# Windowed attention in fp32: edge windows in two groups instead of three, softmax sums inverted on ScalarE by exp and log

## The reference

```python
xn  = layer_norm(x)                              # over the 192 channels
win = pad(xn, 16x16 -> 28x28), cut into 14x14 windows   # 4 windows an image, 196 tokens each
q, k, v = win @ qkv_w                            # 12 heads of 16 channels
s   = (q * 16**-0.5) @ k.T + rel_h(q)[.., :, None] + rel_w(q)[.., None, :]
out = softmax(s, axis=-1) @ v
x   = x + out @ proj_w + proj_b
x   = x + gelu(layer_norm(x) @ fc1_w + fc1_b) @ fc2_w + fc2_b
```

## Time and profile before

| | |
|---|---|
| three runs | 332.98, 334.4, 335.4 us; median 334.4 |
| the profiled execution | 337.13 us; its span in the profile 335.3 us |
| granted clock of TensorE, mean | 0.98 |
| busy share of the span | PE 95%, DVE 57%, ACT 43%, POOL 30% |
| chain that ended last | PE 86%, DVE 7%, ACT 4%, DMA 2% |
| attention blocks in the span | about 7 to 142 us and 163 to 300 us |

### The profile page before, as it was taken

How to read it: one execution, slowest core, us unless ns; L and a number is a source line. 1 busy time by engine, 2 the same in 40 slices (tenths; PEclk the granted TensorE clock), 3 DMA queues, 4 the chain that set the end, 5 groups by cost and what they waited for, 6 DMA issues and landing times.

```text
span 335.3 us, 9323 instructions
## 1 busy us (share of the span) xinstructions
PE 319.6 (95%) x3886; PEld 239.4 (71%) x3886; DVE 190.3 (57%) x457; ACT 143.7 (43%) x312; POOL 102.0 (30%) x215
## 2 busy tenths in 40 slices
PE   6999997999998999999999999799999899999997
PEld 3447686887876439977855769578887644998576
DVE  4473784877867400136674578587785920335572
ACT  3277136554556522024247515655455455002430
POOL 3000553487551049100000066277663104000000
PEclk9599998999999999999999999799999999999999
DMA  7973000000031103020021100000000000000002
GB/s 203 383 269 68 15 7 16 8 10 5 5 86 43 25 0 118 2 70 2 0 96 20 37 4 12 14 9 6 5 4 3 3 0 0 2 0 2 0 2 94
DMA packets 10268, 13.81 MB, mean 41 GB/s; under 512 B 3505, under 2 KB 8337, under 8 KB 10226
## 3 DMA queue, kind: packets, MB, share of 16 engines
q1 hardware_dynamic: 9602, 13.12, 12.5%
q10 hardware_dynamic: 624, 0.09, 0.2%
HBM read 10.95 MB, written 0.79 MB: 35 GB/s over the span
## 4 chain that ended last, share of the span: by engine, by line
PE 86%; DVE 7%; ACT 4%; DMA 2%; issue 1%; ACTq 0%; DVEq 0%
PE banks L1034 13%; PE banks L1006 12%; PE banks L1128 10%; PE banks L1146 9%; PE banks L962 6%; PE banks L1054 6%; PE banks L925 6%; PE banks L896 3%; PE banks L1312 2%; PE banks L885 2%; PE banks L1159 2%; PE banks L1206 2%; PE banks L938 2%; DMA slot_cols<-in_slot_cols 2%; ACT arena L1398 1%; PE banks L1176 1%
## 5 line engine op out<-in xcount | busy, mean ns | idle before, releaser
L1398 ACT ACTIVATE arena<-banks 128x392 f32<-128x392 f32 (+1 forms) x120 | 50.0, 469 | 44.0 <-PE banks L1034 44.0
L1585 DVE TENSOR_REDUCE negmax<-banks 128x4 f32<-128x784 f32 (+1 forms) x52 | 46.7, 897 | 17.5 <-PE banks L1006 17.0
L1006 PE MATMUL banks<-attention_arena 32*128 32x196 f32 x384 | 50.7, 365 | 0.9 <-DVE negmax L1581 0.4
L1034 PE MATMUL banks<-attention_arena 32*128 32x196 f32 x384 | 48.8, 351 | 0.4 <-ACT arena L1398 0.4
L1034 PE MATMUL banks<-attention_arena,keys 32*128 32x196 f32 x384 | 45.7, 332 | 0.0
L1006 PE MATMUL banks<-keys,attention_arena 32*128 32x196 f32 x384 | 45.5, 331 | 0.0
L1034 PEld LDWEIGHTS banks<-attention_arena 32*128 32x128 f32 x384 | 31.5, 191 | 7.0 <-issue 5.2
L1128 PE MATMUL banks<-yT,fc 128*128 128x512 f32 (+1 forms) x96 | 33.3, 607 | 0.0
L1006 PEld LDWEIGHTS banks<-keys,attention_arena 32*128 32x128 f32 x384 | 33.0, 190 | 0.0
L1034 PEld LDWEIGHTS banks<-attention_arena,keys 32*128 32x128 f32 x384 | 33.0, 190 | 0.0
L1006 PEld LDWEIGHTS banks<-attention_arena 32*128 32x128 f32 x384 | 29.9, 190 | 3.7 <-DVE negmax L1581 1.9
(11 more groups left out here) (181 smaller groups left out, 583.2 us busy)
## 6 DMA issues: line engine op xcount, KB each, us to landing
fc<-in_fc SPq DMA_DIRECT2D x2, 768.0 KB, 5.0
fc<-in_fc SPq DMA_DIRECT2D x2, 576.0 KB, 5.6
attention_arena<-negmaxT SPq DMA_DIRECT2D x68, 1.0 KB
rel<-in_rel SPq DMA_DIRECT2D x2, 448.0 KB, 5.9
x_tok<-in_x SPq DMA_DIRECT2D x4, 192.0 KB, 4.4
inverse<-in_inverse SPq DMA_DIRECT2D x1, 768.0 KB
inverse<-in_space_back SPq DMA_DIRECT2D x1, 768.0 KB, 3.9
qkv<-in_qkv SPq DMA_DIRECT2D x1, 576.0 KB, 3.8
```

The lines of the kernel that those rows point to most:

```text
L1006: ins = mm(o, asking, asked, start=not with_rel, stop=bool(with_rel))
L1034: last = mm(m.bank[4 + j][key_rows(b), cols * tile:cols * (tile + 1)], keys_of(slot, b, j, tile)[with_rel], queries_of(slot, b, j, tile)[w ...
L1398: run(m.probsT[keys, n % P_RING, j, 0:cols], m.bank[4 + j][keys, 0:cols], ACT.Exp).then_inc(s.probs, 1)
L1585: dve.tensor_reduce(at[rows, 4 * part:4 * part + 4].rearrange("k (j a) -> k j a", a=2), m.banks[rows, 2 * part:2 * part + 2, 0:2 * keys].r ...
```

## The change

1. **Edge groups.** The six edge units make two groups of three units (`PER_GROUP`), so there are 14 groups: n = 8 and 9 are edges, n = 10 to 13 slot 2. An edge group's `turn` and `score` have six steps, its `weigh` 12 matmuls; matmuls in all are as many as before. `OUT_AT` follows, and the projections stand in the same order as before.
2. **Inverse on ScalarE.** `take_logs` takes Ln of the SBUF copy with a scale and a bias per partition, which leaves the logarithm of the sum in the sum rows and 0 in the others; `invert` takes Exp of minus that, with a bias of 0 or -1e30 per partition. VectorE's `move_inverses` is one stream shuffle that swaps the 16-row halves. So value rows hold the inverse and the other rows 0, and GpSimd's masking goes: `divide` has one instruction for slots 0 and 2, two for slot 1. An edge group with units of both kinds has Ln and Exp in two parts.
3. **Tables.** One set with Exp and Ln is preloaded per attention block; the root of the norm becomes Exp(-0.5 Ln(var)), and VectorE's reciprocal goes. Gelu's table stays.
4. **Padding rows later.** VectorE turns at the end of n = 1, takes maxima at n = 2, sums at n = 3, adds at n = 4, turns back in the middle of n = 5; ScalarE's padding exponential stands at the end of n = 2, the logarithm at the end of n = 3; GpSimd's `shift_pads` behind `divide(0)`, `pad_rows` behind `divide(2)`.
5. **Loads.** `slot_cols` gets a semaphore of its own; TensorE's first transposes wait for `ident` alone.

```diff
 GROUPS = [(slot, b) for slot in range(2) for b in range(IMAGES)]
-GROUPS += [(slot, EDGES) for slot in range(SLOTS)]
+GROUPS += [(third, EDGES) for third in range(UNITS // PER_GROUP)]
 GROUPS += [(SLOTS - 1, b) for b in range(IMAGES)]
...
+def key_tiles(b):
+    return 2 if b < EDGES else PER_GROUP
+def steps_of_group(n):
+    return 2 * key_tiles(GROUPS[n][1])
...
+        def value_parts(n):
+            if GROUPS[n][1] < EDGES:
+                return [(VALUE_HALF[GROUPS[n][0]], slice(0, 1))]
+            own = [[at for at, u in enumerate(units(n)) if VALUE_HALF[unit_slot(u)] == half] for half in range(2)]
+            return [(half, slice(at[0], at[-1] + 1)) for half, at in enumerate(own)]
...
                 edge(0)
-                shift_pads()
                 edge(1)
-                pad_rows()
                 for n in range(N_GROUPS):
                     divide(n)
+                    if n == 0:
+                        shift_pads()
+                    elif n == 2:
+                        pad_rows()
                     if n == 1:
                         edge(2)
...
-                    pe.wait_ge(ident_loaded, 16 * 2)
+                    pe.wait_ge(ident_loaded, 16)
...
             def root(ln, g):
                 act.wait_ge(ln.stats, variances_taken(g))
-                run(m.std[:, 4 * g:4 * g + 4], m.var[:, 4 * g:4 * g + 4], ACT.Sqrt).then_inc(ln.std, 1)
+                own = slice(4 * g, 4 * g + 4)
+                run(m.std[:, own], m.var[:, own], ACT.Ln).then_inc(ln.std, 1)
+                act.wait_ge(ln.std, logged(g))
+                run(m.rstd[:, own], m.std[:, own], ACT.Exp, scale=-0.5).then_inc(ln.std, 1)
...
-                load_table(ACT.Sqrt)
+                act.preload_act_table_set("natural_log_exp_and_others")
...
+                def take_logs(n):
+                    act.wait_ge(s.pv_out, n + 1)
+                    for half, at in value_parts(n):
+                        ins = run(in_parts(m.log[:, n % 2], n)[:, at], in_parts(m.o[:, n % 2], n)[:, at], ACT.Ln,
+                                  scale=c["slot_cols"][:, SLOTS + 1 - half:SLOTS + 2 - half], bias=c["slot_cols"][:, SLOTS + half:SLOTS + half + 1])
+                    ins.then_inc(s.inverted, 1)
+                def invert(n):
+                    act.wait_ge(s.inverted, sums_logged(n))
+                    if n >= 2:
+                        act.wait_ge(s.inverses_moved, n - 1)
+                    for half, at in value_parts(n):
+                        ins = run(in_parts(m.recip[:, n % 2], n)[:, at], in_parts(m.log[:, n % 2], n)[:, at], ACT.Exp, scale=-1.0,
+                                  bias=c["slot_cols"][:, 2 * SLOTS + 1 + half:2 * SLOTS + 2 + half])
+                    ins.then_inc(s.inverted, 1)
...
                         for j in (2 * pair, 2 * pair + 1):
                             run(m.probsT[keys, n % P_RING, j, 0:cols], m.bank[4 + j][keys, 0:cols], ACT.Exp).then_inc(s.probs, 1)
+                            if n > 0 and j == 2 and not last_scored(n):
+                                take_logs(n - 1)
                         if n > 0 and pair == last_scored(n):
                             take_weighed(n - 1)
-                    if n == 0:
+                    if n > 0:
+                        if last_scored(n):
+                            take_logs(n - 1)
+                        invert(n - 1)
+                    if n == 2:
                         act.wait_ge(edge_rows, edge_row(l, "shifted"))
                         run(m.padexp[:], m.padexp[:], ACT.Exp, scale=4.0).then_inc(edge_rows, 1)
-                    elif n == 1:
+                    elif n == 3:
                         act.wait_ge(edge_rows, edge_row(l, "summed"))
                         run(m.padlog[:], m.padsum[:], ACT.Ln).then_inc(edge_rows, 1)
-                load_table(ACT.Sqrt)
                 take_weighed(N_GROUPS - 1)
+                take_logs(N_GROUPS - 1)
+                invert(N_GROUPS - 1)
                 root(s.ln[1], 0)
...
+                def move_inverses(n):
+                    ring = n % 2
+                    dve.wait_ge(s.inverted, inverted(n))
+                    if n >= 2:
+                        dve.wait_ge(s.weighed, attended(n - 2))
+                    dve.stream_shuffle(in_parts(m.inverse[:, ring], n), in_parts(m.recip[:, ring], n), OTHER_HALF).then_inc(s.inverses_moved, 1)
...
-                turn_rows()
                 take_max(2 * FIRST)
-                take_pad_max()
                 for n in range(N_GROUPS):
+                    if has_score(n):
+                        take_max(2 * (n + AHEAD) + 1)
+                    if 2 <= n <= N_GROUPS - 2:
+                        move_inverses(n - 2)
+                    if n == 5:
+                        turn_rows_back()
                     if n + AHEAD + 1 < N_GROUPS:
                         take_max(2 * (n + AHEAD + 1))
+                    if n == 1:
+                        turn_rows()
+                    elif n == 2:
+                        take_pad_max()
+                    elif n == 3:
+                        sum_pads()
+                    elif n == 4:
+                        log_pads()
+                    if not has_score(n):
+                        move_inverses(n - 1)
+                        add_output(n + AHEAD - N_GROUPS)
+                        take_stats(s.ln[1], n + AHEAD - N_GROUPS)
+                move_inverses(N_GROUPS - 1)
+                normalise(wl, s.ln[1], add_output, EPS[l], 4, 9, taken=2)
```

More of the change, by code:

```diff
@@ L79 @@
 VALUE_HALF = (0, 1, 0)
+OTHER_HALF = [(n + HD) % GROUP for n in range(GROUP)]
 def _places():
@@ L141, in _slot_columns @@
     out[ONE_ROW, 2 * SLOTS] = 1.0
+    for half in range(2):
+        out[HD * half:HD * (half + 1), 2 * SLOTS + 1 + half] = -BIG
     return np.tile(out, (4, 1))
@@ L303, in edge_masked, with edge_ready @@
     return 2 * slot + 1
-def edge_ready(slot):
-    return 2 * slot + 2
+def edge_ready(n):
+    return 2 * unit_slot(units(n)[-1]) + 2
 ROW_STEPS = dict(right_copied=1, low_copied=1, turned=1, largest=2, shifted=2, raised=1, summed=2, logged=1, scaled=1, filled=PADS, back=1)
@@ L359, in divided @@
 def divided(n):
-    return sum((1, 2, 0)[slot] for slot, _ in GROUPS[:n]) + 1
+    return sum(slot == 1 or b == EDGES for slot, b in GROUPS[:n]) + 1
 def max_landed(n):
@@ L561, in row, with queries_of, keys_of @@
             return slice(GROUP * j, GROUP * (j + 1))
-        def queries_of(slot, b, j, tile):
+        def queries_of(n, j, tile):
+            slot, b = GROUPS[n]
             if b < EDGES:
                 return inner(m.q[row(j), slot])[:, b], inner(m.r[row(j), slot])[:, b]
-            return m.edgeQ[row(j), slot, tile], m.edgeR[row(j), slot, tile, 0:EDGE_REAL]
-        def keys_of(slot, b, j, tile):
+            u = units(n)[tile]
+            return m.edgeQ[row(j), u], m.edgeR[row(j), u, 0:EDGE_REAL]
+        def keys_of(n, j, tile):
+            slot, b = GROUPS[n]
             if b < EDGES:
@@ L754, in attention @@
                     for slot in range(SLOTS):
[L755 removed]
+                        for to, of in zip(in_pieces(m.edgeR[:, 2 * slot + e], e), pieces(m.r[:, slot], e)):
                             ins = pool.tensor_copy(to, of)
@@ L795, in divide @@
                     slot, b = GROUPS[n]
-                    cols, ring = weighed_cols(b), n % 2
-                    pool.wait_ge(s.inverted, inverses_turned(n))
-                    own = c["slot_cols"][:, SLOTS + slot:SLOTS + slot + 1]
-                    o, part, inverse = m.o[:, ring, 0:cols], m.part[:, ring, 0:cols], m.inverse[:, ring, 0:cols]
-                    if b < EDGES:
-                        places = [inner(m.oT[:, slot // 2])[:, b]]
-                        split = lambda ap: [ap.rearrange("k (r w) -> k r w", r=WIN)]
-                    else:
-                        places = [p for e in range(2) for p in pieces(m.oT[:, slot // 2], e)]
-                        split = lambda ap: [p for e in range(2) for p in in_pieces(ap[:, EDGE_REAL * e:EDGE_REAL * (e + 1)], e)]
-                    if slot == 2:
-                        for to, of, by in zip(places, split(o), split(inverse)):
-                            ins = pool.tensor_tensor(to, of, by, ALU.mult)
-                        ins.then_inc(s.weighed, 1)
+                    ring = n % 2
+                    pool.wait_ge(s.inverses_moved, n + 1)
+                    if b == EDGES:
+                        divide_edges(n, ring)
+                        return
+                    to, shape = inner(m.oT[:, slot // 2])[:, b], lambda ap: ap[:, 0:MAIN_KEYS].rearrange("k (r w) -> k r w", r=WIN)
+                    o, part, inverse = shape(m.o[:, ring]), shape(m.part[:, ring]), shape(m.inverse[:, ring])
+                    if slot != 1:
+                        pool.tensor_tensor(to, o, inverse, ALU.mult).then_inc(s.weighed, 1)
                         return
@@ L1033, in turn @@
                     for j in heads:
```

(8 more changed lines are left out.)

237 lines of the change are left out of this document (108 added, 129 removed).

## The result

Four runs of the changed kernel took 347.48 us at the median (344.45 to 347.53) against 334.9 us before (332.98 to 336.02, four runs): ratio 1.036, 95% interval 1.0284 to 1.0435. The change makes the kernel slower by 12.6 us; forecast were 346.4. The profiled execution took 347.53 with a span of 345.7, against 337.13 and 335.3 before, so the two traces are 10.4 us apart.

A forecast was written before the change was run, and what follows sets the result against it. TensorE, 95% busy, bounds the kernel through its waits. Per layer 13.7 us added less 7.5 gives +6.2; twice +12.4, less 0.45 at the start, +12.0: 349.1, scaled by 0.8% to 346.4 us, range 333 to 352.

The forecast's parts named there:

- The stalls: Moved padding rows: waits delay weighings by +2.95 us (end of n = 2), +0.83 (n = 3) and +2.78 (n = 5) per layer.
- Part 1: ScalarE's added log and inverse: each of five ordinary groups +0.29 us, 1.45 per layer; edge groups also longer.
- The clock: After TensorE idles at n = 3 and n = 5, the clock falls, costing 0.95 and 1.4 us: +2.35 per layer.
- rival (c): The clock holds through the new stalls: 341.7 us; chance 0.12.
- The end of attention: Tail of each layer: Ln, Exp and shuffle precede VectorE's statistics, so fc1 starts later: +1.6 us.
- the lost group: Three edge groups become two: one group goes, -3.5 us, with +0.3 for poor fit, per layer.
- the two terms +0.96 and +0.8: Edge groups' doubled Ln and Exp delay weighings: +0.96 us at n = 10, +0.8 at n = 11, per layer.
- The removed table loads: The hole around the padding's logarithm, with its clock fall, goes: -4.1 us per layer.
- (a): The padding chain stays hidden, with no waits at n = 2 and n = 5: 330.3 us, faster; chance 0.14.
- (b): ScalarE's additions hide in its idle time: +2.1 us a layer, 338.1 us; chance 0.12.
- (d): The clock falls in attention's tail as well: 1.7 us more per layer, 349.8 us; chance 0.13.
- (e): The table set is not kept, so each group reloads tables: over 70 us more; chance 0.02.

The follow-up runs named there:

- Experiment 1: Changed kernel with its padding chain back in the kernel before's places on VectorE, ScalarE and GpSimd: 334.4 us.
- experiment 7: Changed kernel with the padding chain in its old places, except the turn back of the padding rows, left late in group 5: 341.52 us.
- Experiment 2: Changed kernel with the log of the sums directly behind the copy, ahead of the third exponential instead of the fourth: 345.5 us.
- experiment 6: Changed kernel with padding chain in old places, log directly behind the copy, and edge units in three groups of two: 331.65 us.
- Experiment 4: Kernel before with one edit, preloading the table set that holds both log and exponential: 329.26 us.
- experiment 3: Changed kernel with both the padding chain in its old places and the log directly behind the copy: 329.94 us.
- experiment 5: Changed kernel with padding chain in old places, log behind the copy, and at attention's end the variance's log ahead of the last inverses: 327.59 us.

## Why the prediction was right

Direction and size held: +12.0 us of span were forecast, 10.4 came; by the medians it was 12.6. The two long stalls are the forecast's mechanism and carried it; that the total came so close is partly luck, since the errors of the terms cancel: in these traces the ordinary and stalled groups were 1.4 us too low, the clock 2.2 and the ends of attention 0.7 too high. Term by term, in span of the two traces:

| stretch | forecast | layer 1 | layer 2 |
|---|---|---|---|
| start and padding exponential, layer 1 | -0.65 | -0.75 | |
| passes 2 to 9 without clock | +3.91 | +4.67 | +4.57 |
| clock | +2.35 | 0 | +2.50 |
| pass 10 to the next stage | -0.04, +0.16 | -0.42 | -0.17 |

(The first row holds a start that varies by itself. The transposes started at 6.68 instead of 6.95, 0.27 earlier and not 0.45, with no wait for slot_cols.)

**The stalls** were forecast as they came. Passes 3, 4 and 5 were to last 6.60, 4.48 and 6.43 before the clock, and lasted 6.55, 4.44 and 6.67. Experiment 1 takes them away, experiment 7 gives one of them back alone. The shuffle, which no row of before had, took 0.37 where I put 0.36.

**The ordinary groups were undersized.** Part 1 took +0.29 for each of five, 3.94 from weighing to weighing; the mean of the five in layer 1 is 4.14. The durations were right (log 0.54 where I had the row of 539 ns, spacing 0.44 to 0.45 as taken; inverse 0.45, spacing 0.35 against 0.34). The step that failed was where the lateness bites: I let the next group's first exponential decide the weighing, and gave TensorE's second pair, which I had at 1.75 instead of 1.31, no say. The profile after shows it from 82.01 to 83.00: behind a restart the weighing comes 0.95 to 0.99 later, not the half pair of 0.65. With my own 1.75 that gives 2.70 to 2.74 for the weighing and 4.13 to 4.17 for the period, against 4.16 measured. Experiment 2 confirms it: the same work with the log ahead of the third exponential gives 3.92 to 3.98 in passes 7 to 9, and 3.81 to 3.92 in layer 2.

**The clock** was right in size and wrong in frequency. 2.35 was taken for each layer; layer 2 lost 0.94 + 0.58 + 0.98 = 2.50 (passes 4, 5 and 6 against layer 1), layer 1 nothing. Experiment 7's trace lost in both layers, experiment 2's in both. The changed kernel's four executions have mean granted clocks of 0.99 (the traced one), 0.98, 0.99 and 0.98: none is at 1.00, and two are below the traced one, whether by falls in the attention or by a low clock in the start is not known. A term of this kind is a chance and should have been entered as one; rival (c) described one layer of the traced run.

**The end of attention** and the lost group came out 0.3 to 0.4 better. From pass 10 to the last weighing 1.15 and 1.14 us went; the stage behind lost 0.73 and 0.97, not 1.6: fc1 does start 7.02 behind the last weighing instead of 5.83, but a part of this is made up later. Two things in this sum were not seen. GpSimd's division holds output projections, against "worth 0" for a cover of two groups: the chain that ended last has it at 99.59 and the first projection behind it at 100.34, after log, inverse and shuffle from 98.05 on. (The 0.9 of the L943 row of waits is the projection behind the last weighing, which is not on that chain.) And I credited the lost group with a whole period, 3.5 less 0.3; experiment 6 measures 1.4 to 1.5 for it with log and exponential included, so the two terms +0.96 and +0.8 of the wide groups belong to it, and net of them the sum's 1.44 was right.

**The removed table loads** were worth 4.1 per layer in the sum. Experiment 4 gets 3.44 and 3.70 for them and the clock behind them. By the Trainium skill, "ScalarE: Activation LUTs", *What ACT_TABLE_LOAD costs*, a drain comes with each switch; by it this term would have been near 7 a layer, as an estimate; experiment 4's 3.44 and 3.70 speak against it, and the measurement decides.

**The rivals.** (a), a hidden padding chain, is what experiment 1 builds by placement: 334.4, not 330.3, mostly since the ordinary groups are longer than I had them. (b) is out, 4.14 and not 3.65 per group; experiment 3 comes nearest to it with 3.79 to 3.92. (d) is out for this trace, the granted clock from 108 to 111 us is 1.00, and so it is in layer 2's tail (270 to 276 us). (e) is out, there are no loads in the attention.

**The scaling** by 0.8% from the profiled execution to the median took 2.7 us off. The profiled execution before was long for its kernel (337.13 against 332.98 to 336.02 in the others), and the changed kernel's was at its median; that is why the traces are 10.4 us apart and the medians 12.6. So the scaling brought the forecast nearer: 346.4 is 1.1 under the measured median, 349.1 without it would have been 1.6 over.

## What to carry to other kernels

Moving a helper chain later in an in-order queue is not free because each of its pieces is short: count from the link of the chain that cannot start earlier, and name who stands behind every waiting piece. Here such pieces cost 12.8 of the 19.0 us that lie between the changed kernel and the one of experiment 5 behind the first weighing. Work that is put on a half-idle engine goes into the gap in which that engine waits for its input, not between two results that the bounding engine waits for; the log cost 2.3 to 2.7 us a layer for standing one place too late (experiments 1 and 3). And before rewriting a division to save table loads, try the table set that holds both functions: one line gave 1.5%, the rewrite as made lost 3.6% and, reordered as in experiment 5, came out 0.8 us ahead of the one line.

## What the hardware showed unexpectedly

The start of the kernel has more than one length. The first transposes and projections of the changed kernel's trace and of experiment 1's, chain that ended last:

```profile
6.68 1.96 PE banks L932 x8
...
9.62 4.82 PE banks L972 x6
```

```profile
6.76 1.09 PE banks L930 x8
...
8.83 2.81 PE banks L970 x6
```

These are the same instructions. They take 1.7 to 1.8 times as long in one execution as in the other, and the first weighing is 2.6 us apart between experiments 1 and 3 (the traces of experiments 2 and 5 have the short one, those of 3, 4 and 7 the long one, experiment 6 one between). The window tables grant the same clock to both, here the changed kernel and then experiment 1:

```profile
10.00:15.00 5.00, 5.00 (x13) 2.30 (x13) 2.01 (x11) 1.40 (x4) 0.00 (x0) 1.00 1.04 398
```

```profile
10.00:15.00 5.00, 5.00 (x19) 2.17 (x18) 3.14 (x11) 3.28 (x7) 0.00 (x0) 1.00 1.04 410
```

The kernel before shows the same slowness with a clock beside it. Its six projections and its window:

```profile
9.04 5.46 PE banks L925 x6
```

```profile
10.00:15.00 5.00, 5.00 (x10) 2.29 (x9) 1.60 (x10) 1.19 (x3) 0.00 (x0) 0.50 1.02 387
```

Here the granted clock is 0.50, 1.2 GHz, and in experiment 6, whose six projections take 4.40, it is 0.50 from 10 to 12 us. In the other long starts the instructions last about as long while 1.00 is recorded (experiment 4 has 5.20 for the six projections). So a long start looks like time at 1.2 GHz that the clock record does not always show; that is argued from the durations and not shown, and what makes a start long was not tried. It is why the comparisons above go by pieces of the span: a difference of 2.6 us between two traces of this kernel may be the start alone.
